# A pre-norm attention layer on 8 cores: the low half of an elementwise product is split between GpSimd and VectorE

## The reference

```python
x = x + attn(layernorm(x), W_qkv, b_qkv, W_proj, b_proj)     # x: [16, 2048, 1024] f32
x = x + ffn(layernorm(x), Win, bin_, W1, b1, W2, b2, Wout, bout)

# attn: 16 heads of 64; scores q.k / 8, softmax over the allowed j, times v, projected
#   allowed (i, j), j <= i:  j = i, and j = i - 1, i - 2, i - 4, ..., i - 1024
#   (a second rule of the mask only adds pairs with j > i, which the causal cut removes)
# ffn:  s = x @ Win + bin_ ; h = relu(s[..., None] * W1 + b1) ; g = sum_h(h * W2) + b2 ; g @ Wout + bout
```

## Time and profile before

| | us |
|---|---|
| median of 3 runs | 1564.95 |
| lowest and highest of them | 1561.52, 1592.67 |
| the profiled execution, whole | 1565.49 |
| its span, first to last instruction of the slowest core (core 6) | 1563.9 |
| spans of the 8 cores | 1554.7 to 1563.9 |
| mean granted TensorE clock of the cores (share of full speed) | 0.823 to 0.828 |

### The profile page before, as it was taken

One profiled execution on the slowest core, in us unless ns is written; L12 is line 12 of the kernel. 1 busy time (PEld: TensorE's weight loads), 2 busy tenths in 40 slices (PEclk: granted clock), 3 DMA queues, 4 the chain that ended last, 5 costly groups with the idle time before them and its releaser, 6 DMA issues.

```text
span 1563.9 us, 22066 instructions; the slowest of 8 cores (1554.7 to 1563.9 us)
## 1 busy us (share of the span) xinstructions
PE 1122.9 (72%) x6656; PEld 620.8 (40%) x6656; DVE 718.3 (46%) x1944; ACT 401.4 (26%) x899; POOL 292.8 (19%) x329
## 2 busy tenths in 40 slices
PE   0098786887867768678687878777785777867775
PEld 0066352453524435245253535244352433524432
DVE  5245344444545445344454535454444544544444
ACT  0133320323213222032232333131322213213221
POOL 1000202103041050420500020301205114051050
PEclk9999797896968969689698979698796877868866
DMA  9700101001010010100101010101001010010000
GB/s 155 127 1 1 54 1 54 1 1 54 1 54 1 16 40 1 54 1 1 55 1 54 1 54 1 54 1 45 10 1 55 1 55 1 1 54 1 21 8 28
DMA packets 13281, 43.89 MB, mean 28 GB/s; under 512 B 2608, under 2 KB 2864, under 8 KB 13168
## 3 DMA queue, kind: packets, MB, share of 16 engines
q1 hardware_dynamic: 9584, 33.65, 6.0%
q0 software_dynamic: 3584, 8.82, 3.7%
HBM read 34.51 MB, written 16.78 MB: 33 GB/s over the span
## 4 chain that ended last, share of the span: by engine, by line
PE 53%; issue 14%; DVE 13%; POOL 9%; ACT 7%; another core or an unknown queue 2%; DVEq 1%; DMA 1%; POOLq 0%; ACTq 0%; SPq 0%
PE p_o L607 7%; PE p_A L941 6%; PE p_o L661 6%; POOL s_tmpsp L725 5%; PE p_B L941 4%; PE p_A L607 3%; PE p_o L485 3%; POOL s_ebuf L725 3%; PE p_B L607 2%; ACT s_pmask L881 2%; PE p_sc L868 2%; DVE s_xT L493 2%; PE p_sc L874 2%; PE p_B L661 2%
## 5 line engine op out<-in xcount | busy, mean ns | idle before, releaser
L725 POOL TENSOR_TENSOR s_ebuf<-s_qZ,s_kT 64x256 bf16<-64x256 bf16 x136 | 103.1, 758 | 1018.0 <-DVE s_qZ L618 557.5
L607 PE MATMUL p_o<-s_xT,s_wqkv 128*128 128x256 bf16 x1152 | 133.7, 273 | 0.0
L881 ACT ACTIVATE s_pmask<-p_sc 128x512 bf16<-128x512 f32 (+1 forms) x192 | 104.3, 592 | 63.2 <-PE p_sc L874 62.5
L607 PEld LDWEIGHTS p_o<-s_xT,s_wqkv 128*128 128x128 bf16 x1152 | 112.8, 98 | 13.2
L941 PE MATMUL p_A<-s_wproj,s_oT 128*128 128x512 bf16 x256 | 101.1, 567 | 6.8 <-DVE s_oT L493 6.2
L725 POOL TENSOR_TENSOR s_tmpsp<-s_qZ,s_kT 64x256 bf16<-64x256 bf16 x136 | 98.3, 722 | 0.6
L432 ACT ACTIVATE s_xln<-s_x 128x1024 f32<-128x1024 f32 x32 | 33.5, 1049 | 251.5 <-DVE s_stats L429 251.5
L485 PE MATMUL p_sc<-s_identf,s_xln 128*128 128x128 f32 x126 | 32.1, 309 | 87.6 <-DVE s_stats L538 77.5
L607 PE MATMUL p_A<-s_xT,s_wqkv 128*128 128x256 bf16 x512 | 69.5, 274 | 34.1 <-DVE s_qZ L618 21.1
L661 PE MATMUL p_o<-s_wqkv,s_xT 128*128 128x512 bf16 x384 | 91.2, 380 | 0.0
L485 PE MATMUL p_o<-s_identf,s_xln 128*128 128x128 f32 x379 | 71.7, 308 | 27.0 <-DVE s_xln L919 27.0
(11 more groups left out here) (161 smaller groups left out, 1957.1 us busy)
## 6 DMA issues: line engine op xcount, KB each, us to landing
s_x<-x SPq DMA_DIRECT2D x16, 1024.0 KB, 5.2
y<-s_x SPq DMA_DIRECT2D x16, 1024.0 KB, 4.0
s_wqkv<-wqkv POOLq DMA_DIRECT2D x1, 6144.0 KB, 50.2
s_wproj<-wproj POOLq DMA_DIRECT2D x1, 2048.0 KB, 61.1
s_win<-win POOLq DMA_DIRECT2D x1, 128.0 KB, 61.0
s_woutaug<-wout POOLq DMA_DIRECT2D x1, 128.0 KB, 56.8
s_mb<-mb01x POOLq DMA_DIRECT2D x1, 128.0 KB, 56.8
s_identf<-ident SPq DMA_DIRECT2D x1, 64.0 KB, 1.9
```

Of the source, the lines that this page charges most:

```text
L607: t_mm = P.emit("tensor", lambda ec, pb=pb, lhs=lhs, rhs=rhs, dc=dc: ec.matmul(pb[:, 0:CH], lhs, rhs, start=(dc == 0), stop=(dc == NDC - 1 ...
L725: t_e1 = P.emit("gpsimd", lambda ec, elo=elo, qlo=qlo, kap_lo=kap_lo: ec.tensor_mul(elo, qlo, kap_lo), deps=dq + ebuf_rd[es] + (scr_rd if ...
L881: t_exp = P.emit("scalar", lambda ec, pm=pm, scp=scp, width2=width2: ec.activation(pm, scp[:, 0:width2], AF.Exp, bias=-8.0, scale=0.125), ...
```

## The change

The low 64 partitions of each product, until now one POOL multiply, are cut in two. POOL keeps partitions 0 to 31. A new DVE multiply (`t_e2a`) takes partitions 32 to 63, and stands ahead of the DVE multiply of partitions 64 to 127, which stays as it was. The waits on the matmul of two steps before and on readers of the scratch tile move to the new multiply; the old DVE multiply, second in the same queue, waits for q alone. The matmul waits for all three. The lists that guard k and q against being overwritten get the new multiply too. Nothing else is changed.

```diff
-                        kap_lo = kT[0:64, dc * T + t0 + a - o: dc * T + t0 + a - o + w]
+                        kap_lo = kT[0:32, dc * T + t0 + a - o: dc * T + t0 + a - o + w]
+                        kap_md = kT[32:64, dc * T + t0 + a - o: dc * T + t0 + a - o + w]
                         kap_hi = kT[64:128, dc * T + t0 + a - o: dc * T + t0 + a - o + w]
-                        qlo = qZ[0:64, dc * CH + a: dc * CH + a + w]
+                        qlo = qZ[0:32, dc * CH + a: dc * CH + a + w]
+                        qmd = qZ[32:64, dc * CH + a: dc * CH + a + w]
...
-                            elo = ebuf[0:64, a:a + w]
+                            elo = ebuf[0:32, a:a + w]
+                            emd = ebuf[32:64, a:a + w]
                             ehi = ebuf[64:128, a:a + w]
...
                         t_e1 = P.emit("gpsimd", lambda ec, elo=elo, qlo=qlo, kap_lo=kap_lo: ec.tensor_mul(
                             elo, qlo, kap_lo), deps=dq + ebuf_rd[es] + (scr_rd if es == 1 else []))
+                        t_e2a = P.emit("vector", lambda ec, emd=emd, qmd=qmd, kap_md=kap_md: ec.tensor_mul(
+                            emd, qmd, kap_md), deps=dq + ebuf_rd[es] + (scr_rd if es == 1 else []))
                         t_e2 = P.emit("vector", lambda ec, ehi=ehi, qhi=qhi, kap_hi=kap_hi: ec.tensor_mul(
-                            ehi, qhi, kap_hi), deps=dq + ebuf_rd[es] + (scr_rd if es == 1 else []))
+                            ehi, qhi, kap_hi), deps=dq)
...
-                            deps=([t_e1, t_e2, t_bo] + sc_war) if dc == 0 else [t_e1, t_e2])
+                            deps=([t_e1, t_e2a, t_e2, t_bo] + sc_war) if dc == 0 else [t_e1, t_e2a, t_e2])
```

More of the change, by code:

```diff
@@ L720, in build_program @@
                         else:
-                            elo = tmpsp[0:64, VA_W + a: VA_W + a + w]
+                            elo = tmpsp[0:32, VA_W + a: VA_W + a + w]
+                            emd = tmpsp[32:64, VA_W + a: VA_W + a + w]
                             ehi = tmpsp[64:128, VA_W + a: VA_W + a + w]
@@ L737, in build_program @@
                             kv_rd[jt].append(t_e1)
+                            kv_rd[jt].append(t_e2a)
                             kv_rd[jt].append(t_e2)
                         qT_rd.append(t_e1)
+                        qT_rd.append(t_e2a)
                         qT_rd.append(t_e2)
```

## The result

| | kernel before | changed kernel |
|---|---|---|
| median, us | 1565.59 | 1630.87 |
| lowest and highest, us | 1561.52, 1592.67 | 1627.77, 1684.83 |
| ratio, with its 95% interval | | 1.0424 [1.0404, 1.0445] |
| span of the slowest core in the profile, us | 1563.9 | 1627.6 |
| the 14 elementwise stages together, us | 211.5 | 275.4 |

The change makes the kernel 4.2% slower. The highest time of each kernel is a single slow execution (in the 1684.83 us of the changed kernel, four of the cores were granted a clock of 0.75 to 0.76 and the other four 0.81), and the ratio leaves these out. A stage is measured here in the timeline, from the start of its first DVE multiply to the start of the first exponential behind it (before: 745.54 to 764.28). The 14 stages have grown by 63.9 us and the span by 63.7. The 13 stretches between them add up to 1113.8 us before and 1113.9 after.

A forecast was written before the change was run, and what follows sets the result against it. No engine was full; in the elementwise stages POOL's queue and the loop through DVE, POOL and matmul both bound a step at 0.77 us. Forecast: 1565.5 + 61 + 4 = 1630.5, say 1631 us (+4.2%), range 1582 to 1655.

The forecast's parts named there:

- the turn: Elementwise stage: POOL's and DVE's two-input multiplies alternate as whole instructions, POOL's turn about 0.53 us, DVE's about 0.15.
- POOL's multiply at half the partitions: Elementwise step: POOL's multiply of 32 partitions taken to keep 0.66 us; far bound 0.33.
- The rivals with a cheaper POOL: Elementwise steps: POOL's multiply at 0.57 us gives 1584 us (chance 0.07), at 0.33 gives 1530 (chance 0.03).
- The overlap of two multiplies with one start partition: DVE in the stage: starts 0.21 us apart would go; two multiplies then take 0.30 + 0.29.
- The round of three steps: Elementwise stage, laid out by hand: three steps in 3.07 us, 1.02 a step against 0.77 before.
- 244 x 0.25 + 14 x 0.30: Forecast loss: 244 steps each 0.25 us longer (61 us), 14 stage starts each 0.30 later (4 us).
- The near tie: Third step of a round: POOL's multiply may start at 1.63 us, just ahead of the old DVE multiply at 1.66.
- the hand schedule: Starts and ends of the new steps' DVE and POOL multiplies and matmuls, laid out from trace durations: 1.02 us a step.
- leaves POOL idle for its matmul: Stage: the second DVE multiply always falls into a POOL multiply, then POOL waits idle for its matmul; 61 us.
- room for 7.0 us more: Stage of 24 steps: 24 x 0.29 = 7.0 us more DVE time would fit beside 7.41 busy of 18.80; in turns maybe not.
- The rival of turns at full length: Elementwise steps: whole-instruction turns, 0.66 + 0.29 + 0.29 = 1.24 us a step, 119 us more, 1684 us; chance 0.08.
- The clock: PE at 0.50 in the stage and 0.82 behind it; whether more quiet time gives back clock was unknown, nothing taken.

## Why the prediction was right

**The step that carried it.** The price was not in any duration of the trace but in how durations of one instruction differed: 0.66 against 0.77 for POOL, 0.29 against 0.72 for DVE. The two experiments that keep two DVE instructions a step and take the turn away, one by moving POOL's work (1526.15 us) and one by an instruction that takes no turn (1567.66), show that the turn is the cause.

**POOL's multiply at half the partitions.** Taken as unchanged; shown alone in its own experiment (211.6 us of stages against 211.5). The rivals with a cheaper POOL fall with it.

**The new DVE multiply.** 0.28 us where 0.29 was taken, and the next one 0.29 behind it (772.19 and 772.48 in the profile of the changed kernel) where 0.30 was taken. The first matmul of that stage, at 772.92, stands 0.73 behind the first multiply, as laid out. The overlap of two multiplies with one start partition went as forecast; with one start partition throughout, multiplies start 0.21 apart again (710.47 and 710.68 above).

**The round of three steps.** 3.07 laid out, 3.08 measured. 244 x 0.25 + 14 x 0.30 = 65 stands against 63.9 us more in the stages. The near tie fell the way it was laid out, by 0.02 us where the schedule had 0.03. That is no more than the roundings of its terms, so the match to 0.1 us owes something to luck. Had the tie fallen the other way, the hand schedule says 0.95 a step, about 1614 us, still within the range. That order was not tried.

**What was wrong in it.** The text gave as the loss that the blocked multiply leaves POOL idle for its matmul. The kernel with four product tiles refutes that reading: there the wait is for the matmul of four steps before, and the round is no shorter. POOL's 0.82 us idle time is what is left over when DVE, always busy, is late. The lengths came out right because the hand schedule had DVE's queue in it, whichever engine one blames. It also means that DVE's busy time of the kernel before, where there seemed to be room for 7.0 us more, was the wrong measure: one DVE multiply grows from 0.29 to 0.66 or 0.79 merely by being issued into a POOL multiply.

**The rival of turns at full length** would have given 1.24 us a step; 1.02 was measured over a full round. The DVE turn is short, as the trace before showed.

**The clock.** The granted clock stays at 0.50 in the longer stage. The stretch behind it shows 0.77 against 0.82, yet the stretches between stages are as long as before (1113.9 and 1113.8 us). With stages as short as in the kernel with one multiply and four tiles they add up to 1103.9, 10 us less; whether that is the clock or the freed POOL was not separated.

## What to carry to other kernels

Before an instruction is split so that another engine takes a part, look whether the two engines' instructions get longer when they overlap: a row of the same instruction at 0.29 and at 0.72 us is the price, and free busy time does not cover it. Two engines that take turns can be slower than one of them alone: here a step took 0.77 us with both and 0.61 with the same two multiplies on DVE. All the work on DVE in one instruction over all partitions was worth 5.9%, and two more buffers 3.7 points more. Cutting these multiplies by partitions saved no time: DVE's took 0.28 us with 32 partitions and 0.29 with 64 and with 128, POOL's 0.66 alone with 32 and with 64.

## What the runs showed of the hardware that was not expected

A DVE copy of bf16 with every second element of its input took 283 ns for 256 elements and took turns with POOL like a two-input multiply (642 and 755 ns at most). A DVE maximum over the same number of elements took 411 ns (410 to 413 over all 272) and never did.
